# Feed-forward steps of a fused attention block regrouped, with three score banks and an earlier second transpose of maxima

## What is computed

```python
x = x + attn1(conv(x, cond) + b)        # 16 heads of 32, causal, ALiBi bias, out projection
# second attention: x.T as (256 channels, 512 positions), 16 heads of 16, mask = cond
att = einsum('bhqd,bhkd->bhqk', Q, K) * Dh**-0.5 + b
att = softmax(att * m + (1 - m) * -1e30)
y = einsum('bhqk,bhkd->bhqd', att, V)
# feed-forward, whose gate, up and down weights are Catmull-Rom splines of few control points
x = x + (silu(y @ gate_w.T) * (y @ up_w.T)) @ down_w.T
```

## Time and profile before

| | us |
|---|---|
| median of 3 runs | 1317.77 |
| lowest, highest | 1312.59, 1326.76 |
| profiled execution, span and time | 1322.0 |
| TensorE busy in it | 1216.3 |
| VectorE busy | 780.9 |
| ScalarE busy | 507.2 |
| GpSimd busy | 355.0 |

### The profile page before, as it was taken

The page is one execution under the profiler, slowest core; times in us unless marked ns, Lnnn a source line. Parts: engine busy times, 40 slices in busy tenths (PEclk is TensorE's granted clock), DMA queues, the critical chain, the costliest instruction groups (busy, mean ns, idle before and its releaser), DMA issues.

```text
span 1322.0 us, 20809 instructions
## 1 busy us (share of the span) xinstructions
PE 1216.3 (92%) x7400; PEld 672.6 (51%) x7400; DVE 780.9 (59%) x1173; ACT 507.2 (38%) x699; POOL 355.0 (27%) x201
## 2 busy tenths in 40 slices
PE   5685789999999999999999999999999999999988
PEld 4352245554555545555546545555355555465436
DVE  7676644578445882568635783467725675356822
ACT  1131243334533265223633256322552336332572
POOL 3183770092003800075000910048000740000000
PEclk9687689998999999999999999999899989999999
DMA  8989604382226704265044822267042640448024
GB/s 294 279 318 309 175 2 112 139 193 103 49 67 173 238 23 112 98 154 182 14 102 146 208 80 66 53 178 229 23 112 108 167 159 15 100 149 221 36 113 175
DMA packets 81057, 180.89 MB, mean 137 GB/s; under 512 B 14468, under 2 KB 54356, under 8 KB 71284
## 3 DMA queue, kind: packets, MB, share of 16 engines
q1 hardware_dynamic: 70864, 161.56, 42.1%
q10 hardware_dynamic: 8832, 13.91, 3.1%
q0 software_dynamic: 1280, 4.20, 0.9%
HBM read 106.41 MB, written 21.14 MB: 96 GB/s over the span
## 4 chain that ended last, share of the span: by engine, by line
PE 75%; DVE 8%; DMA 6%; POOL 5%; issue 3%; ACT 2%; SPq 1%; ACTq 0%; DVEq 0%; POOLq 0%
PE psum L1181 9%; PE psum L1131 8%; PE psum L955 8%; PE psum L995 5%; PE psum L984 5%; PE psum L973 4%; PE psum L961 4%; DMA products<-in_gu_points 4%; DVE max L863 4%; PE psum L996 4%; PE psum L997 4%; PE psum L1089 4%; PE psum L1100 4%; PE psum L1168 3%; PE psum L1052 3%
## 5 line engine op out<-in xcount | busy, mean ns | idle before, releaser
L863 DVE TENSOR_REDUCE max<-psum 128x1 f32<-128x512 f32 x512 | 327.0, 684 | 111.3 <-PE psum L1131 109.4
L699 ACT ACTIVATE probs<-psum 128x1024 f32<-128x1024 f32 x256 | 248.0, 1022 | 168.2 <-PE psum L1168 166.9
L1131 PE MATMUL psum<-k,q 52*128 52x512 f32 x512 | 186.7, 514 | 28.8 <-DMA k<-low 15.2
L555 POOL TENSOR_TENSOR h<-h_in,tap 128x1024 f32<-128x1024 f32 x7 | 13.3, 1897 | 604.9 <-DVE low L766 604.9
L1131 PEld LDWEIGHTS psum<-k,q 52*128 52x128 f32 x512 | 79.3, 199 | 165.6 <-DVE max L863 129.5
L1181 PE MATMUL psum<-probs,v 128*32 128x512 f32 x1024 | 145.7, 643 | 0.4 <-ACT probs L699 0.3
L1168 PE MATMUL psum<-q,k 54*128 54x512 f32 x512 | 116.8, 452 | 14.7 <-DMA q<-max_l 7.2
L565 POOL TENSOR_TENSOR h<-h,products 128x1024 f32<-128x1024 f32 x49 | 123.5, 2520 | 3.8
L995 PE MATMUL psum<-stack 128*128 128x512 f32 x256 | 113.7, 444 | 0.0
L764 DVE CAST high<-low 128x1024 fp32r<-128x1024 f32 x32 | 25.3, 790 | 148.3 <-ACT low L586 120.6
L955 PE MATMUL psum<-h,qkv_w 128*128 128x256 f32 x448 | 105.9, 390 | 4.1 <-POOL h L565 4.1
(11 more groups left out here) (112 smaller groups left out, 1645.7 us busy)
## 6 DMA issues: line engine op xcount, KB each, us to landing
stack<-wd_sorted SPq DMA_DIRECT2D x64, 1024.0 KB, 6.7
stack<-high SPq DMA_DIRECT2D x128, 128.0 KB, 2.4
stack<-low SPq DMA_DIRECT2D x64, 128.0 KB, 2.4
q<-high SPq DMA_DIRECT2D x128, 64.0 KB, 4.3
k<-high SPq DMA_DIRECT2D x128, 64.0 KB, 2.5
h_in<-in_x_lanes SPq DMA_DIRECT2D x9, 512.0 KB, 3.9
x<-in_x_rows SPq DMA_DIRECT2D x8, 512.0 KB, 7.9
x_scratch<-x SPq DMA_DIRECT2D x8, 512.0 KB, 3.9
```

Of the source, the lines that this page charges most:

```text
L699: nc.scalar.activation(probs[:, u // 2 % 2, u % 2 * 2:u % 2 * 2 + 2, :], psum[:, 2 + u % 2 * 2:4 + u % 2 * 2, :], ACT.Exp)\
L863: nc.vector.reduce_max(max2[:, g, e, i, t:t + 1], psum[:, bank, :], AX_X).then_inc(S["s2_max"], 1)
L1131: nc.tensor.matmul(psum[:, banks[s], :], r(q2[rows, g, i, t * P:(t + 1) * P]), r(k2[rows, g, i, :]), start=True, stop=True).then_inc(S["s2 ...
```

## The change

Within a step TensorE's order is now: first pair of scores, gate_up, second pair, turn, moments, and both down groups one behind the other. Scores 0 to 27 take banks 0, 1 and 5 in turn; bank 5 was a bank of the moments, which from the sixth on all use bank 2 and so wait for one copy more. VectorE takes three maxima ahead of gated where it took two, and turn(0) now stands behind the fourth. Behind the window, round 1 is written out: the shifted products 0 to 3, turn(1) straight behind them and into bank 0, that of score 31, where it was bank 7 behind the totals; then one score, the first values, and the other three scores. VectorE takes total 0, the turned maxima, total 1, and then the round's four maxima. Score 33, the next in bank 0, waits until the turned maxima are read, and scores in bank 7 wait for the totals.

```diff
-SCORE_BANKS = [s % 2 for s in range(WINDOW_SCORES)]
+def least_recent(banks, free):
+    return min(free, key=lambda x: len(banks) - 1 - banks[::-1].index(x) if x in banks else -1)
+
+
+SCORE_BANKS = []
+for _s in range(WINDOW_SCORES):
+    SCORE_BANKS.append(least_recent(SCORE_BANKS, (0, 1, 5) if _s < WINDOW_SCORES - 4 else (0, 1)))
 for _k in range(1, 1 + (NS - WINDOW_SCORES) // 4):
     for _s in range(4):
         _free = (0, 1) if _k in TURN_AT or _k in OUT_AT else (7, 0, 1)
-        SCORE_BANKS.append(min(_free, key=lambda x: len(SCORE_BANKS) - 1 - SCORE_BANKS[::-1].index(x)
-                               if x in SCORE_BANKS else -1))
+        SCORE_BANKS.append(least_recent(SCORE_BANKS, _free))
...
-Z_BANKS = (2, 5)
+Z_BANKS = (2, 5, 2, 5, 2, 2, 2, 2)
 GU_BANK, SUM_BANK = 3, 6
-TURN_BANKS = (Z_BANKS[0], 7, 7, 7)
+TURN_BANKS = (Z_BANKS[0], SCORE_BANKS[WINDOW_SCORES - 1], 7, 7)
+BEHIND_TURN = SCORE_BANKS.index(TURN_BANKS[1], WINDOW_SCORES)
...
-                nc.scalar.activation(z[:, n % 2, :], psum[:, Z_BANKS[n % 2], 0:L], ACT.Copy).then_inc(S["z_out"], 1)
+                nc.scalar.activation(z[:, n % 2, :], psum[:, Z_BANKS[n % NT], 0:L], ACT.Copy).then_inc(S["z_out"], 1)
...
                 for n in range(NT + 1):
                     for s in window_pair(n, 0):
                         maximum(s)
+                    for s in window_pair(n, 1)[:1]:
+                        maximum(s)
                     if not first and n + 1 < NT:
                         gated(b, n + 1)
+                    for s in window_pair(n, 1)[1:]:
+                        maximum(s)
                     if n == TURN_STEP:
                         turn(0)
-                    for s in window_pair(n, 1):
-                        maximum(s)
                     if not first and n + 1 < NT:
                         rest(b, n + 1)
                 if not first:
-                    totals(b)
-
-                for k in range(1, ROUNDS + 1):
+                    totals(b, (0,))
+                turn(1)
+                if not first:
+                    totals(b, (1,))
+                for s in (*round_scores(1, 0), *round_scores(1, 1)):
+                    maximum(s)
+
...
-                    pe.wait_ge(S["z_out"], fed(b, "z_out", n - 1))
+                    pe.wait_ge(S["z_out"], fed(b, "z_out", n - 1 if n <= 2 * AHEAD else n))
...
                             wait("aug_rows", 64)
                     if s < len(set(banks[:WINDOW_SCORES])):
                         wait("v2_out", CT)
-                    elif last_in_bank is None:
+                        if banks[s] == Z_BANKS[1] and not first:
+                            pe.wait_ge(S["z_out"], fed(b, "z_out", 2 * AHEAD))
+                    elif last_in_bank is None and not first:
+                        pe.wait_ge(S["sum_out"], fed(b, "sum_out", LT))
+                    elif last_in_bank is not None:
+                        wait("s2_max", last_in_bank + 1)
+                    if s == BEHIND_TURN:
                         wait("max2_low", 2)
-                    else:
-                        wait("s2_max", last_in_bank + 1)
...
-                        pe.wait_ge(S["z_out"], fed(b, "z_out", NT - 1))
+                        pe.wait_ge(S["z_out"], fed(b, "z_out", NT))
+                    elif g == 1:
+                        wait("max2_low", g)
                     elif g < NG - 1:
                         wait("max2_low", g)
-                        if g == 1 and first:
-                            wait("k2_out", LT)
-                        elif g == 1:
+                        if not first:
                             pe.wait_ge(S["sum_out"], fed(b, "sum_out", LT))
...
-                        if first:
-                            wait("s2_max", WINDOW_SCORES - 4)
-                        else:
+                        wait("s2_max", WINDOW_SCORES - 4)
+                        if not first:
                             pe.wait_ge(S["inter_out"], fed(b, "inter_out", NT))
...
-                for n in range(NT + 1):
+                for n in range(NT):
+                    for s in window_pair(n, 0):
+                        scores(s)
                     if not first and n + 1 < NT:
                         gate_up(b, n + 1)
+                    for s in window_pair(n, 1):
+                        scores(s)
+                    if n == TURN_STEP:
+                        turn(0)
                     if not first and n == 0:
                         wait("v2_out", CT)
                         moments(b, AHEAD)
                     if not first and n + AHEAD + 1 < NT:
                         moments(b, n + AHEAD + 1)
-                    for s in window_pair(n, 0):
-                        scores(s)
-                    if n == NT:
-                        shifted(0)
-                    if n == TURN_STEP:
-                        turn(0)
                     if not first and n:
                         down(b, n - 1, 1)
-                    for s in window_pair(n, 1):
-                        scores(s)
-                    if n == NT:
-                        shifted(1)
-                    if not first and n < NT:
+                    if not first:
                         down(b, n, 0)
 
-                for k in range(1, ROUNDS + 1):
+                for s in window_pair(NT, 0):
+                    scores(s)
+                shifted(0)
+                if not first:
+                    down(b, NT - 1, 1)
+                for s in window_pair(NT, 1):
+                    scores(s)
+                shifted(1)
+
+                shifted(2)
+                shifted(3)
+                turn(1)
+                for s in round_scores(1, 0)[:1]:
+                    scores(s)
+                values2(0)
+                for s in (*round_scores(1, 0)[1:], *round_scores(1, 1)):
+                    scores(s)
+
+                for k in range(2, ROUNDS + 1):
```

More of the change, by code:

```diff
@@ L786, in rest, with totals @@
                     .then_inc(S["inter_low"], 1)
-            def totals(b):
+            def totals(b, parts=range(LT)):
                 dve.wait_ge(S["xr_loaded"], fed(b, "xr_loaded", 16))
-                for s in range(LT):
+                for s in parts:
                     dve.wait_ge(S["sum_ready"], fed(b, "sum_ready", s + 1))
@@ L972, in moments @@
                         cols = slice((2 * (n % NT) + s // 2) * ZR, (2 * (n % NT) + s // 2 + 1) * ZR)
-                        last = nc.tensor.matmul(psum[s * ZR:(s + 1) * ZR, Z_BANKS[n % 2], 0:L], zt[:, c, cols],
+                        last = nc.tensor.matmul(psum[s * ZR:(s + 1) * ZR, Z_BANKS[n % NT], 0:L], zt[:, c, cols],
                                                 y[:, c, :], start=i == 0, stop=i == 1, skip_group_check=True)
@@ L1207, in batch @@
                         moments(b, n + AHEAD + 1)
-                    for s in window_pair(n, 0):
-                        scores(s)
-                    if n == NT:
-                        shifted(0)
-                    if n == TURN_STEP:
-                        turn(0)
                     if not first and n:
                         down(b, n - 1, 1)
-                    for s in window_pair(n, 1):
-                        scores(s)
-                    if n == NT:
-                        shifted(1)
-                    if not first and n < NT:
-                        down(b, n, 0)
-                for k in range(1, ROUNDS + 1):
+                    if not first:
+                        down(b, n, 0)
+                for s in window_pair(NT, 0):
[14 more added lines that the diff above has]
+                    scores(s)
+                for k in range(2, ROUNDS + 1):
                     if k < ROUNDS:
```

## The result

| | before | changed |
|---|---|---|
| median, us | 1316.48 (4 runs) | 1337.89 (4 runs) |
| lowest, highest | 1312.59, 1326.76 | 1334.50, 1340.31 |
| profiled execution, span | 1322.0 | 1338.4 |

The ratio is 1.0128, 95% interval 1.0085 to 1.017: slower by 1.3%. The time lies 14 us above the forecast's 1323.5 and 4 us above the top of its range, 1334.

The account below looks back on a forecast made before the run. TensorE, busy 1216.3 of 1322.0 us, was taken as the bound. Six batches of +1.5 gave +9, the last +0.2, the clock -5.5: +3.6, so 1325.6 against the profiled execution, 1321.4 against the median, middle 1323.5 us; range 1304 to 1334.

Parts of the forecast that it names:

- A: Whole kernel: the forecast itself, 1323.5 us, from 1318 to 1330; chance 0.48.
- The fourth scores behind the subtraction: Window steps: a subtraction held by GpSimd delays the next step's fourth score, 3.0 us a batch, bounds 1 and 4.5.
- The walk: One inner batch timed step by step: fourth-score delays of 0.52, 1.12, about 0, 1.10 and 0.26, sum 3.0 us.
- Then about 0: The walk's third delay of a fourth score, after +0.52 and +1.12: about 0 us.
- The check by the mean: Same delays from averages: about 1.1 us of GpSimd's instruction left, the part over 0.60 averaging 0.6 us, five times.
- The first score behind its stack copy: Window's start: first scores wait for the last stack copy, landing 2.3 us after issue; +1.5 us in six batches.
- The saving of the grouping: Steps 1 to 7, down products in one piece of twelve: -3.1 us a batch, 0.3 either way.
- The last batch: Batch without convolution on GpSimd: 2.1 - 3.1 + 1.1 + 0.1 = +0.2 us.
- Behind the window: New order at the window's end: +0.1 us a batch, bounds -0.36 and +0.4.
- The clock: Granted clock: 11.5 us regained behind the window, +6 for falls at window starts at about even odds; together -5.5.
- B: Rival: subtractions mostly meet GpSimd's gaps or hold TensorE less, 1 us a batch; about 1309 us (1300 to 1314); chance 0.25.
- C: Rival: idle time at the window's start drops the clock each batch, waits at 4.5 us; 1338 (1331 to 1345); chance 0.15.

Follow-up runs that it names:

- the new steps with the old end: Changed kernel with its regrouped steps and three banks, but the end of the window as before: 1342.18 us, 1.0161 against the kernel before.
- the short convolution: GpSimd's convolution products and additions on 8 of 256 columns only: 1312.48 us (0.9899) in the changed kernel, 1313.35 us (0.9924) in the kernel before.
- the moved subtractions: Changed kernel with VectorE's subtraction of steps 2 to 7 behind the next step's first maximum: 1314.05 us, 0.993 against the kernel before.
- the new start: Changed kernel with gate_up(2) and moments(4) ahead of step 1's scores: 1336.32 us (1.0106); with subtractions of steps 2 to 7 moved too, 1310.13 us (0.9912).

## Why the prediction was off in size

It forecast a small loss, 1323.5, and held slower by over 1% for 0.19 likely; the time lies above A's own range, too, which ended at 1330. The signs and places of its terms hold; three sizes do not. The profiled execution is 1338.4 us, where the sum gave 1325.6.

- **The fourth scores behind the subtraction: +3.0 forecast, +4.2 measured,** each batch. The walk gave 0.52, 1.12, 0, 1.10, 0.26 for steps 2 to 6; the rows give 0.41, 1.12, 1.56, 1.12, 0. "Then about 0" is the step that failed. By the walk's own times that subtraction is due at 424.70 + 2 x 5.63 + 0.52 + 1.12 + 5.05 = 442.65, and the kernel before shows a gap of 0.07 us just ahead of that on GpSimd:

```profile
440.65 1.91 POOL L562 TENSOR_TENSOR products<-h_in,tap 128x1024 f32<-128x1024 f32 x1
...
442.63 2.71 POOL L565 TENSOR_TENSOR h<-h,products 128x1024 f32<-128x1024 f32 x1
```

The walk took the gap as met. GpSimd's row and the end of step 0 both came 2.81 us later in the changed kernel, so 445.60 there is 442.79 here: 0.14 us later than walked, and 0.16 behind the start of the addition. So it took the longest time in this kernel, 2.76. Due times that are good to 0.1 or 0.2 us can't place an instruction in a gap of 0.07. The 1.10 of the step behind it was walked from that 0, so its agreement with 1.12 is luck. The check by the mean was off too: with 1.28 us free and an end 0.54 us behind GpSimd's, the part over 0.74 counts and not the part over 0.60, which makes 0.5 us and 2.4 for five. The forecast's upper bound, 4.5, was nearer than its value.
- **The first score behind its stack copy: 1.5 forecast, 1.7 measured.** Issue plus 2.3 us was right (here 425.17 + 2.3 = 427.47), and the 0.2 from landing to the score's start was taken as 0.1.
- **The saving of the grouping: 3.1 forecast, 2.8 measured,** worked out as 1.71 + 4.21 - 3.14. Steps without a wait take 5.65 us (5.63 forecast), 4.66 and 4.64 (4.66, 4.63), but step 7 takes 4.67, where 4.44 was forecast. That sum has a slip: a fourth score at 1.27, 0.43 to the down products and 2.95 make 4.65. A fourth score that waited is still 0.42 us ahead of what follows it (465.08 to 465.50).
- Together the window is 3.1 us longer in each of six batches instead of 1.4, +18.7 us instead of +8.4. This is 10.3 of the 12.8 us between 1325.6 and 1338.4; the rest is the other stages (below). The last batch, forecast +0.2 in all, shows +0.07 in the window: there the grouping's saving pays for the wait for the copy and no more.
- **Behind the window: +0.1 forecast, +0.1 measured** (5.20 against 5.10).
- **The clock: -5.5 forecast, -5.7 measured behind the window, by two errors that cancel.** The loss there was 11.5 us before, as taken, but half of it stayed (four falls of seven), and the +6 for falls at the window's start did not come: none in seven. Such falls do happen: in two batches of the new steps with the old end and in one each of two other kernels, right behind that idle stretch. There the step took 7.10 to 7.22 us, and 7.04 with the short convolution, instead of 5.65. Together with the changed kernel itself that is 4 of 28 batches, where even odds were given. The other stages show one fall more than before, +2.5 us, which the forecast left at 0; that part differs from one execution to the next.
- **The rivals.** B, the gaps are met, is ruled out: none of rest(2) to rest(5) took under 1.41 us in an inner batch. C had the right total, 1338, with waits near its upper end (4.2 against 4.5), but its mechanism, the clock at the window's start, was not in this profile. The time of C came from A's mechanism at C's size.

VectorE held until GpSimd's instruction ends is what every row shows: ends at 434.39, 441.15 and 448.36, which is 0.55, 0.55 and 0.56 behind GpSimd's 433.84, 440.60 and 447.80. The Trainium skill ("SBUF — State Buffer", section "SBUF: two separate sides") states that the two engines' shared port pair is an exclusive lock, held for a whole instruction; the trace agrees. The short convolution shows that meeting GpSimd's long instructions is the whole of the loss, within its interval of 0.4%, and the moved subtractions remove as much with the convolution in place.

What stays open: whether the 1.2 us that the new start wins in a batch could be kept, if the down weights and the subtraction that step 5 waits for came sooner. That wasn't tried. Why the clock falls less often behind the new end is not shown either; the counts are.

## What to carry to other kernels

Where VectorE can be locked out by GpSimd, an instruction's place in VectorE's order can matter more than its length, as here: put the work that the critical engine waits for ahead of the one that can be held, and spend the slack behind it. Before a regrouping is costed by what it saves on the bottleneck, count the slack of every step of the chain beside it (here 2.85 us before, 1.11 after, against holds of up to 2.76), and take the upper bound of the hold for each step, since delays move the next meeting too. When steps are anchored to an engine that keeps its own pace, time won ahead of an anchor is given back at it.

## What the runs showed of the hardware

- A GpSimd instruction takes 0.3 us longer when it follows one for which a subtraction was held: 2.70 us at 440.68, where the same addition takes 2.36 to 2.40 when none was. It goes the other way round as well: in the kernel before, the addition that began at 447.40, just behind the subtraction's start at 447.36, took 2.88 us.
- VectorE is not held when one operand comes from PSUM: gated at 442.87 takes 0.67 us, beside GpSimd's addition that runs until 443.38, and three maxima from 441.07 take 1.87 us beside the same one. Of the kinds seen here only the subtraction, with both operands in SBUF, is held.
- The granted clock can fall behind one idle stretch of TensorE of 1.4 to 2.0 us and not behind another of the same length: in 4 of 6 inner batches behind the 1.36 us of step 2 with the new start, in 4 of 28 behind the 1.5 to 2.0 us at the window's start. Three of those four follow one of the seven longest stretches (1.88 us or more), one follows the 21 shorter ones (1.72 or less). Length alone doesn't settle it, since the 1.36 us was followed by falls more often than those.
